# The last layer's norm and router logits, written out for all sixteen tiles

## The reference, cut to what matters

```python
def _layernorm(x, axis=-1, eps=1e-05):
    m = jnp.mean(x, axis=axis, keepdims=True)
    v = jnp.var(x, axis=axis, keepdims=True)
    return (x - m) / jnp.sqrt(v + eps)
...
    def _L3_ffn_ref(hidden_states, gate_w, w1, w2, w3):
        ...
        x = hidden_states.reshape(-1, H)
        router_logits = x @ gate_w.T
        probs = jax.nn.softmax(router_logits.astype(jnp.float32), axis=-1)
        top_w, top_i = jax.lax.top_k(probs, TOP_K)
        top_w = top_w / jnp.sum(top_w, axis=-1, keepdims=True)
        ...
        for e in range(E):
            h = jax.nn.silu(x @ w1[e].T) * (x @ w3[e].T)
            out = out + w_dense[:, e:e + 1] * (h @ w2[e].T)
        return out.reshape(B, S, H)
...
    x = x + _L3_ffn_ref(_layernorm(x, axis=-1), L3_ffn_gate_w, L3_ffn_w1, L3_ffn_w2, L3_ffn_w3)
```

## Time and profile before

| what | value |
|---|---|
| three runs | 2675.97, 2686.22, 2693.60 us (median 2686.22) |
| the profiled execution, its own time | 2672.96 us |
| its span, first to last instruction | 2671.2 us |
| mean granted TensorE clock | 0.900 |
| TensorE busy | 2229.9 us, 83% of the span |
| VectorE busy | 1538.1 us, 58% |
| ScalarE busy | 1238.1 us, 46% |
| GpSimd busy | 253.7 us, 9% |
| the first block of the last phase | from about 2192 to 2242.7 us |

### The profile page before, as it was taken

The page is one execution under the profiler, slowest core; times in us unless marked ns, Lnnn a source line. Parts: engine busy times, 40 slices in busy tenths (PEclk is TensorE's granted clock), DMA queues, the critical chain, the costliest instruction groups (busy, mean ns, idle before and its releaser), DMA issues. The chain is left out here.

```text
span 2671.2 us, 47176 instructions
## 1 busy us (share of the span) xinstructions
PE 2229.9 (83%) x18862; PEld 1628.9 (61%) x18865; DVE 1538.1 (58%) x2902; ACT 1238.1 (46%) x2456; POOL 253.7 (9%) x239
## 2 busy tenths in 40 slices
PE   7979798999798887899779888749889764899996
PEld 5634366566454555556556566538656544899996
DVE  3534576555555555777555666475466535667773
ACT  2246534443553222555435644624368411566663
POOL 0010000000200000000000000000100000344442
PEclk9989999899898988999989999869889755899998
DMA  2010010000100002000010010000000022666663
GB/s 89 30 61 9 2 60 32 0 1 1 68 2 30 0 0 62 1 1 1 1 28 9 0 55 0 0 32 0 0 1 2 33 67 73 205 202 197 206 212 104
DMA packets 62537, 125.37 MB, mean 47 GB/s; under 512 B 15960, under 2 KB 45273, under 8 KB 62201
## 3 DMA queue, kind: packets, MB, share of 16 engines
q1 hardware_dynamic: 53530, 110.83, 12.3%
q0 software_dynamic: 8832, 12.06, 2.2%
HBM read 109.18 MB, written 15.80 MB: 47 GB/s over the span
## 5 line engine op out<-in xcount | busy, mean ns | idle before, releaser
L248 PE MATMUL ps<-all_xnT,all_w 128*128 128x512 f32 (+2 forms) x496 | 261.0, 665 | 9.9 <-DVEq L1991 6.3
L256 PE MATMUL ps<-ffn_xh,ffn_wh 128*128 128x256 f32 x644 | 184.8, 287 | 1.5 <-DVE ffn_xl L4018 1.5
L256 PE MATMUL ps<-ffn_xh,ffn_wl 128*128 128x256 f32 x644 | 183.1, 284 | 0.0
L256 PE MATMUL ps<-ffn_xl,ffn_wh 128*128 128x256 f32 x644 | 183.0, 284 | 0.0
L210 POOL TENSOR_TENSOR all_rstd<-all_mv,all_cst 128x4 f32<-128x4 f32 x52 | 10.6, 204 | 1803.1 <-DVE all_mv L193 1742.7
L248 PEld LDWEIGHTS ps<-all_xnT,all_w 128*128 128x128 f32 (+2 forms) x496 | 95.4, 207 | 121.5 <-issue 109.2
L4013 DVE TENSOR_TENSOR ffn_wl<-ffn_fresh,ffn_wh 128x1792 fp32r<-128x1792 f32 x69 | 139.4, 2023 | 26.2 <-ACT ffn_wh L3891 21.1
L2008 DVE SCALAR_TENSOR_TENSOR attn_xc<-attn_cx,all_w,attn_xc 128x512 f32<-128x512 f32 (+1 forms) x144 | 107.5, 750 | 66.2 <-ACT attn_xc L1858 62.8
L263 PE MATMUL ps<-all_w,all_xnT 128*128 128x256 f32 (+3 forms) x384 | 116.5, 450 | 13.2 <-ACT ffn_vec L2583 8.6
L256 PEld LDWEIGHTS ps<-ffn_xh,ffn_wh 128*128 128x128 f32 x644 | 124.4, 193 | 1.9 <-DVE ffn_xl L4018 1.9
L256 PEld LDWEIGHTS ps<-ffn_xl,ffn_wh 128*128 128x128 f32 x644 | 124.3, 193 | 0.0
(11 more groups left out here) (439 smaller groups left out, 5653.4 us busy)
## 6 DMA issues: line engine op xcount, KB each, us to landing
ffn_fresh<-in_l3f_w SPq DMA_DIRECT2D x69, 896.0 KB, 4.6
all_w<-in_ctxT SPq DMA_DIRECT2D x8, 512.0 KB, 6.2
xattn_ctxT<-in_ctxT SPq DMA_DIRECT2D x8, 512.0 KB, 4.5
all_x<-in_x_rows SPq DMA_DIRECT2D x4, 512.0 KB, 7.3
all_x<-x_seq SPq DMA_DIRECT2D x4, 512.0 KB, 5.3
all_w<-in_ctx SPq DMA_DIRECT2D x4, 512.0 KB, 4.1
all_w<-in_l2x_o SPq DMA_DIRECT2D x1, 2048.0 KB, 9.4
all_w<-in_l2f_up SPq DMA_DIRECT2D x1, 2048.0 KB, 9.1
```

The lines of the kernel that those rows point to most:

```text
L248: last = pe.matmul(out, w[:, c, n0:n1], k.xnT[:, c, a:b], start=start and c == 0, stop=stop and c == KC - 1)
L256: last = pe.matmul(out, a, b, start=start and n == 0, stop=stop and n == 2)
```

## The change

The loops of the first block are written out, and each engine gets an order of its own over all sixteen tiles. Statistics, mean, variance and rstd have room for all sixteen tiles (`bn`, `mv`, `rstd`), the turned tiles for two groups (`xnT_all`), and the transposes two pairs of PSUM banks (0 and 1, 2 and 3). All logits go to bank 4, 8 columns for each tile.

- VectorE makes the statistics of all tiles, then all means and variances, then scales all tiles, straight into `xn_all`. It waits once for the logits of all groups and copies them with one instruction.
- GpSimd makes rstd group by group.
- TensorE runs `turn(0)`, `turn(1)`, `score(0)`, `turn(2)`, `score(1)`, `turn(3)`, `score(2)`, `score(3)`.
- ScalarE copies only the turned tiles; the copy L3726 is gone.
- SyncE stores the scaled rows in four DMAs of 512 KB, each when its group is scaled.

The choice behind it and the second block are as they were.

```diff
--- before.py
+++ after.py
@@ -3689,24 +3689,45 @@
     with ExitStack() as prep:
         k.phase_ctx = prep
         xn_all = k.sb("xn_all", [P, BATCH, D])
-        norm = Norm(k, (0, 1))
+        xnT_all = k.sb("xnT_all", [P, 2, KC, T])
+        bn = k.sb("bn", [P, BATCH, 6])
+        mv = k.sb("mv", [P, BATCH, 2])
+        rstd = k.sb("rstd", [P, BATCH, 1])
+        XT = [k.psum[0:2], k.psum[2:4]]
+        logits = k.psum[4]
         gate_loaded = Signal(k, "gate_loaded")
-        logits_psum = Signal(k, "logits_psum", 1)
-        logits_ready = Signal(k, "logits_ready", 1)
-        kept = Signal(k, "xn_kept", 1)
+        stats_ready = Signal(k, "stats_ready")
+        var_ready = Signal(k, "var_ready")
+        eps_added = Signal(k, "eps_added")
+        rstd_ready = Signal(k, "rstd_ready")
+        xn_ready = Signal(k, "xn_ready")
+        xnT_psum = Signal(k, "xnT_psum")
+        xnT_ready = Signal(k, "xnT_ready")
+        logits_psum = Signal(k, "logits_psum")
+        logits_ready = Signal(k, "logits_ready")
         rows_stored = Signal(k, "rows_stored")
         zeros_set = Signal(k, "zeros_set")
         shifted = Signal(k, "shifted")
         exps_ready = Signal(k, "exps_ready")
         dummies = Signal(k, "dummies")
         steps2 = Signal(k, "choice_steps")
+
+        def of_group(g):
+            return slice(g * TG, (g + 1) * TG)
+
         with nc.Block() as block:
             @block.gpsimd
             def _(pool):
                 pool.memset(zeros[:, :], 0.0).then_inc(zeros_set.sem, 1)
                 pool.memset(logit[:, :, EXPERTS:], -3e38).then_inc(dummies.sem, 1)
-                with pool.Fori(0, GROUPS) as i:
-                    norm.pool(pool, i)
+                for g in range(GROUPS):
+                    at = of_group(g)
+                    pool.wait_ge(*var_ready(0, g + 1))
+                    pool.tensor_tensor(rstd[:, at, :], mv[:, at, 1:2], k.c["eps5"][:, 0:TG].unsqueeze(2),
+                                       ALU.add).then_inc(eps_added.sem, 1)
+                    pool.wait_ge(*eps_added(0, g + 1))
+                    pool.tensor_tensor(rstd[:, at, :], rstd[:, at, :], k.c["exp_m05"][:, 0:TG].unsqueeze(2),
+                                       ALU.pow).then_inc(rstd_ready.sem, 1)
 
             @block.sync
             def _(sp):
@@ -3715,39 +3736,80 @@
                 sp.wait_ge(*zeros_set(0, 1))
                 sp.dma_start(acc[ROWS:ROWS + P, :], zeros[:, :]).then_inc(rows_stored.sem, 16)
                 sp.dma_start(rows[ROWS:ROWS + P, :], zeros[:, :]).then_inc(rows_stored.sem, 16)
-                sp.wait_ge(*kept(0, GROUPS))
-                sp.dma_start(rows[0:ROWS, :].rearrange("(b p) d -> p b d", p=P), xn_all[:, :, :]).then_inc(rows_stored.sem, 16)
-                sp.wait_ge(*rows_stored(0, 64))
+                for g in range(GROUPS):
+                    at = of_group(g)
+                    sp.wait_ge(*xn_ready(0, 2 * g + 2))
+                    sp.dma_start(rows[g * T:(g + 1) * T, :].rearrange("(b p) d -> p b d", p=P),
+                                 xn_all[:, at, :]).then_inc(rows_stored.sem, 16)
+                sp.wait_ge(*rows_stored(0, 48 + 16 * GROUPS))
 
             @block.scalar
             def _(act):
-                with act.Fori(0, GROUPS) as i:
-                    norm.scalar(act, i)
-                    act.activation(xn_all[:, bass.ds(i * TG, TG), :], k.xn[:, :, :], ACT.Copy).then_inc(kept.sem, 1)
+                for g in range(GROUPS):
+                    for u in range(2):
+                        act.wait_ge(*xnT_psum(0, 2 * g + u + 1))
+                        if g >= 2:
+                            act.wait_ge(*logits_psum(0, g - 1))
+                        act.activation(xnT_all[:, g % 2, :, u * 2 * P:(u + 1) * 2 * P],
+                                       XT[g % 2][u][:, :].rearrange("p (c t) -> p c t", c=KC),
+                                       ACT.Copy).then_inc(xnT_ready.sem, 1)
                 act.wait_ge(*shifted(0, 1))
                 act.activation(chosen[:, :, :], chosen[:, :, :], ACT.Exp).then_inc(exps_ready.sem, 1)
 
             @block.tensor
             def _(pe):
+                def turn(g):
+                    for u in range(2):
+                        pe.wait_ge(*xn_ready(0, 2 * g + u + 1))
+                        if g >= 2:
+                            pe.wait_ge(*xnT_ready(0, 2 * (g - 2) + u + 1))
+                        for v in range(2):
+                            for c in range(KC):
+                                at = c * 2 * P + v * P
+                                last = pe.transpose(XT[g % 2][u][:, at:at + P],
+                                                    xn_all[:, g * TG + 2 * u + v, c * P:(c + 1) * P], k.c["ident"])
+                        last.then_inc(xnT_psum.sem, 1)
+
+                def score(g):
+                    pe.wait_ge(*xnT_ready(0, 2 * g + 2))
+                    for t in range(TG):
+                        at = (g * TG + t) * EXPERTS
+                        for c in range(KC):
+                            last = pe.matmul(logits[:, at:at + EXPERTS], xnT_all[:, g % 2, c, t * P:(t + 1) * P],
+                                             gate[:, c, :], start=c == 0, stop=c == KC - 1)
+                    last.then_inc(logits_psum.sem, 1)
+
                 pe.wait_ge(*gate_loaded(0, 16))
-                with pe.Fori(0, GROUPS) as i:
-                    norm.tensor(pe, i)
-                    pe.wait_ge(*norm.xnT_ready(i, 2))
-                    for t in range(TG):
-                        last = project_rows(pe, k, k.psum[2][:, t * EXPERTS:(t + 1) * EXPERTS], gate, 0, EXPERTS, t)
-                    last.then_inc(logits_psum.sem, 1)
+                turn(0)
+                for g in range(GROUPS):
+                    if g + 1 < GROUPS:
+                        turn(g + 1)
+                    score(g)
 
             @block.vector
             def _(dve):
-                with dve.Fori(0, GROUPS) as i:
-                    norm.vector(dve, i)
-                    dve.wait_ge(*logits_psum(i, 1))
-                    for t in range(TG):
-                        last = dve.tensor_copy(logit[:, i * TG + t, 0:EXPERTS],
-                                               k.psum[2][:, t * EXPERTS:(t + 1) * EXPERTS])
-                    last.then_inc(logits_ready.sem, 1)
-                    dve.wait_ge(*logits_ready(i, 1))
-                    dve.wait_ge(*kept(i, 1))
+                for g in range(GROUPS):
+                    for b in range(g * TG, (g + 1) * TG):
+                        last = dve.bn_stats(bn[:, b, :], k.x[:, b, :])
+                    last.then_inc(stats_ready.sem, 1)
+                for g in range(GROUPS):
+                    dve.wait_ge(*stats_ready(0, g + 1))
+                    if g == GROUPS - 1:
+                        dve.memset(k.spare[:, :], 0.0)
+                    for b in range(g * TG, (g + 1) * TG):
+                        last = dve.bn_aggr(mv[:, b, :], bn[:, b, :])
+                    last.then_inc(var_ready.sem, 1)
+                for g in range(GROUPS):
+                    dve.wait_ge(*rstd_ready(0, g + 1))
+                    for b in range(g * TG, (g + 1) * TG):
+                        last = dve.tensor_scalar(xn_all[:, b, :], k.x[:, b, :], mv[:, b, 0:1], rstd[:, b, 0:1],
+                                                 ALU.subtract, ALU.mult)
+                        if b % 2 == 1:
+                            last.then_inc(xn_ready.sem, 1)
+                dve.wait_ge(*logits_psum(0, GROUPS))
+                dve.tensor_copy(logit[:, :, 0:EXPERTS], logits[:, 0:BATCH * EXPERTS].rearrange("p (b e) -> p b e", e=EXPERTS))\
+                   .then_inc(logits_ready.sem, 1)
+                dve.wait_ge(*logits_ready(0, 1))
                 chain = Chain(dve, steps2)
                 dve.wait_ge(*dummies(0, 1))
                 for b in range(BATCH):
```

## The result

The changed kernel takes 2661.66 us (median of 20 runs, 2653.51 to 2676.09) against 2677.10 us before (median of 20, 2672.28 to 2693.60). The ratio is 0.9937 with a 95% interval of 0.9920 to 0.9954, which is 17 us less, between 12 and 21; the two medians lie 15.4 us apart. The forecast was 14.6 us less. The time lies inside the predicted range, and within 1% of before.

A forecast was written before the change was run, and what follows sets the result against it. The prediction took an unoverlapped chain of engines, each idle while the next works, to bound the block. MAX8 at 2221.6 instead of 2236.18 saves 14.6 us, stores and next block adding 0: 2686.22 becomes 2671.6, range 2655 to 2686.

The forecast's parts named there:

- (1): VectorE, block's start: statistics for all sixteen tiles first delay the first scaling by 3.9 us, paid once.
- (2): GpSimd's roots running beside VectorE's scaling: taken to cost 0, upper bound 3.2 us.
- Rival B: VectorE and GpSimd exclude each other fully during roots and scaling: 11.4 us saved, 2674.8; chance 0.12.
- (3): TensorE's transposes and products run densely for 20.9 us, plus 0.2 us for hand-overs, ending at 2221.1.
- (4): Logits to SBUF in one copy: 0.5 us, give or take 0.2, from TensorE's end to MAX8, instead of 0.92.
- (5): Rows stored by groups without ScalarE's copies: hidden, 0 us; the old store would have become the shorter block's end.
- (6): The next block starts 14.6 us earlier, otherwise the same; the clock's rise there may shift it plus or minus 1 us.
- TensorE's clock: Granted clock in the stage stays at 0.50 (1.2 GHz) despite dense TensorE work; no rise forecast.
- Rival A: One short rise of TensorE's clock, 3.4 us, in the stage: 2.8 us more, 17.4 in all, 2668.8; chance 0.22.
- D: Row stores become the block's end, 3.1 us after VectorE's: 11.5 us saved in all, 2674.7; chance 0.03.
- E: Code loading of written-out instructions stops TensorE, 1.6 us per fetch: 7.8 us slower, 2694.0; chance 0.02.
- F: TensorE still waits 0.7 us for ScalarE before each score: 2.8 us lost, 11.8 saved, 2674.4; chance 0.05.

The follow-up runs named there:

- e1: Changed kernel with each group taken through all engines before the next begins, as in the old loop; 42.9 us from first bn_stats to first MAX8.
- e11: Changed kernel with statistics and scaling done two groups at a time instead of all statistics first; 23.8 us from first bn_stats to first MAX8.
- e8: Changed kernel plus a GpSimd memset of a spare tile beside the first group's scaling; 30.0 us from first bn_stats to first MAX8.
- e2: Changed kernel with ScalarE's row copies and the single 2048 KB store behind them put back; 25.4 us from first bn_stats to first MAX8.
- e3: Changed kernel with one 2048 KB store of the scaled rows instead of four; 25.4 us from first bn_stats to first MAX8.
- e5: Changed kernel profiled once more, with nothing altered; 25.4 us from first bn_stats to first MAX8.
- e4: Changed kernel without look-ahead: TensorE does turn(g), then score(g); 32.7 us from first bn_stats to first MAX8.
- e6: Changed kernel with TensorE's work ordered by half groups, one half ahead; 28.3 us from first bn_stats to first MAX8.
- e7: Changed kernel with all 32 transposes before all products and room for four turned groups; 22.5 us from first bn_stats to first MAX8.
- e12: Changed kernel with statistics, scaling and TensorE's order in twos, room for four turned groups; 18.9 us to first MAX8, kernel 2661.82 us.
- e10: Changed kernel with statistics made one group ahead of the scaling instead of all first; 26.2 us from first bn_stats to first MAX8.

## Why the prediction was right, point by point

- *A chain of engines, none overlapped, is what bounds the block*: right. e1 puts the order back and loses 17.5 of the 18.7 us, about 14.4 of them to waits that return and 3.1 to the rise that goes.
- (1) *Fill of 3.9 us*: VectorE scaled 7.0 us behind the first bn_stats (2202.49 - 2195.48) instead of 3.2, 3.8 us. e11 shows that it was avoidable.
- (2) *Roots beside the scaling*: taken at 0 on the path, measured 0.3 us over sixteen tiles, and TensorE's first 32 records have no gap. The row at 331 us was the right one to take. Rival B is out.
- (3) *TensorE dense, 20.9 us and 0.2 for hand-overs*: the pace was sized a little high. Without a rise the same order took 20.3 us from first to last (e8), instead of 21.1.
- (4) *Logits' copy, 0.5 us from TensorE's end to MAX8*: 0.37 (2220.53 to 2220.90).
- *The sum.* Without the rise TensorE would have worked 20.3 us (e8) instead of 17.2, so MAX8 would have come at 28.5: 15.6 us saved, where 14.6 were forecast. The 1.0 us between them is 0.8 of (3), and 0.1 each of (1) and (4).
- (5) *Stores hidden*: right, but its reason was not. The four stores landed in 3.2 us each (median), and nothing waited for them. The sentence that the old store "would have become the end of the shorter block" left out that ScalarE's last copy moves forward with the pipeline (e2, e3).
- (6) *Next block the same within 1 us*: half right. The first expert matmul came 46.0 us behind MAX8, 45.3 before, and all profiles lie between 45.3 and 46.1. The whole part behind MAX8 was 3.1 us longer in this pair of profiles, of which 1.1 us go with the later rise of the clock, as (6) allowed, and 2.0 with a wait for a gather that it had not thought of and that e5 doesn't show. Its factor of 0.55 came from records of 8 and 32 columns and not from "such" ones as the experts'; theirs, of 256 columns, start 0.21 us apart at half clock and 0.12 at full (2284 to 2287 in the profile of before), which is near it.
- *TensorE's clock*: the step that failed. I took L4064's row for the stage, and the stage had a short rise of its own. The row that I held against it I had also misread. There the clock rose when only two of the eight transposes had begun:

```profile
2185.60:2189.60 4.00, 3.78 (x8) 0.50 0.00 0
2189.60:2190.00 0.40, 0.33 (x2) 0.50 0.00 0
2190.00:2193.40 3.40, 0.91 (x8) 1.00 0.06 8
```

  What came before that rise were L3626's eight records of 256 columns, so it is no precedent for a run of transposes. Rival A was held at 0.22 and happened in both profiles of the changed kernel. Its size was off too: at full clock a record takes half the time (32 records in 3.30 us), not 0.55 of it, since my 0.55 came from groups of sixteen, whose time holds the longer last record; the rise was worth 3.1 us instead of 2.8. With it the block's gain is 18.7 us, where A gave 17.4. The measured 17 us, with 12 to 21 in its interval, cannot tell the forecast from A. That the kernel's time came so near to 14.6 is in part luck: the block gave 4.1 us more than forecast, 3.1 of it by a rise that the forecast had left out, and the part behind MAX8 and the scatter between runs hide that.
- *Rivals D, E and F*: no store is late, TensorE's row has no gap put down to issue, and the look-ahead works; F's price was 4.1 us, not 2.8 (e4). E's figure for a fetch, 1.6 us, is no measured price of one, and no run here shows a stop for code.

## What to carry to other kernels

When four engines pass one group around in a loop, the idle time of the one with the most work bounds the gain; write its dense work and its fill down separately, since the first is a floor and the second can be shortened with two groups of work ahead instead of all. Before crediting a removed copy or a finer store, move everything else forward on paper first: here both were hidden already. And read the granted clock of each stretch before booking a difference on a wait: the same 96 records, without a gap on TensorE, took 20.1 us in e6's order, 17.2 in the changed kernel's and 14.2 in e7's and e12's, and 20.3 in the changed kernel's order when it began 1.4 us later.

## What the runs showed of the hardware

- Inside the block the granted clock rose only in kernels that run sixteen or more transposes in a row, and in none with at most eight (before, e1, e4, e6, e10), in stretches of 3.4 us or twice that, beginning 3.5 to 4.1 us behind the first transpose of the run. Ahead of the block it also rose behind eight records of 256 columns (L3626). It did not always rise: the same sixteen, begun 9.3 us instead of 4.3, 7.9 or 11.7 us behind the block's start, brought none. What decides that stays open.
- A GpSimd memset of 1.81 us held VectorE's tensor_scalar up for 1.4 us; an eps addition and a power of 128 x 4 elements, 0.2 and 1.0 us alone, cost VectorE about 0.1 us together, and the power itself took 1.03 to 1.21 us.
- A wait for ScalarE's copy cost TensorE more than its idle time in the trace: 1.0 us, of which the brackets show 0.69 (e4).
